# Query maxima of two attentions: split by query rows and turned in the score ring, in place of turned first and split after

## The reference

```
scores = q @ k.T * scale            # 1024 x 1024 for each batch and head
scores = scores + bias, causal mask # layer 1 only
attn   = softmax(scores, axis=-1)
y      = attn @ v                   # then a 128 x 128 output projection
```

## Time and profile before

| | before |
|---|---|
| time, median of 3 runs | 1030.89 us (1030.69 to 1034.01) |
| time of the profiled execution | 1036.33 us |
| its span in the profile | 1034.5 us |
| busy share of the span: PE, DVE, ACT, POOL | 87%, 78%, 59%, 19% |
| mean granted TensorE clock | 0.921 |
| L1025 DVE reductions of the first pass | 640, 488.3 us busy |
| L982 ACT exponentials of the second pass | 896, 436.3 us busy |
| L794 PE turns of maxima | 32 |
| L1000, L1002 DVE splits | 32 each |
| L560 transfers of maxima rows | 128 of 2.0 KB |

### The profile page before, as it was taken

How to read it: one execution, slowest core, us unless ns; L and a number is a source line. 1 busy time by engine, 2 the same in 40 slices (tenths; PEclk the granted TensorE clock), 3 DMA queues, 4 the chain that set the end, 5 groups by cost and what they waited for, 6 DMA issues and landing times. The chain is left out here.

```text
span 1034.5 us, 22166 instructions
## 1 busy us (share of the span) xinstructions
PE 899.6 (87%) x8501; PEld 458.8 (44%) x8501; DVE 805.0 (78%) x1600; ACT 612.7 (59%) x1280; POOL 199.8 (19%) x249
## 2 busy tenths in 40 slices
PE   5589999999899987984689999999998898777788
PEld 3212222222222223883345445555535666645568
DVE  7789999999899861656787787778862587799687
ACT  3228888888888786543236677766754346433552
POOL 2202033331302110540200011103010023133221
PEclk9659999999999898996779999999969998988899
DMA  2632435524426321111645753334301000000001
GB/s 77 186 87 61 118 95 124 101 70 94 99 76 146 96 60 19 50 35 49 177 99 141 188 104 87 88 73 88 68 7 30 6 1 2 1 0 1 4 6 36
DMA packets 62678, 73.71 MB, mean 71 GB/s; under 512 B 21144, under 2 KB 46865, under 8 KB 62559
## 3 DMA queue, kind: packets, MB, share of 16 engines
q1 hardware_dynamic: 48222, 49.23, 19.8%
q0 software_dynamic: 8576, 17.86, 7.2%
q10 hardware_dynamic: 5776, 5.22, 1.6%
HBM read 44.59 MB, written 18.16 MB: 61 GB/s over the span
## 5 line engine op out<-in xcount | busy, mean ns | idle before, releaser
L1025 DVE TENSOR_REDUCE a_negmax<-a_mbank 128x1 f32<-128x1024 f32 (+4 forms) x640 | 488.3, 818 | 72.7 <-PE a_mbank L829 35.2
L982 ACT ACTIVATE a_probs<-a_ebank 128x512 f32<-128x512 f32 (+3 forms) x896 | 436.3, 554 | 163.6 <-PE a_ebank L859 85.5
L850 PE MATMUL a_ebank<-b_moving,b_still 50*128 50x512 bf16 (+4 forms) x1280 | 270.0, 368 | 19.4 <-ACT a_probs L982 10.6
L821 PE MATMUL a_mbank<-a_moving,a_still 48*128 48x512 bf16 (+4 forms) x1280 | 263.3, 377 | 22.5 <-DVE a_negmax L989 9.8
L873 PE MATMUL a_acc<-a_probs,a_slot_v 128*32 128x512 f32 (+3 forms) x1792 | 224.9, 575 | 1.1 <-ACT a_probs L982 1.1
L850 PEld LDWEIGHTS a_ebank<-b_moving,b_still 58*64 58x64 bf16 (+1 forms) x1280 | 85.0, 102 | 254.0 <-ACT a_probs L982 198.6
L821 PEld LDWEIGHTS a_mbank<-a_moving,a_still 56*64 56x64 bf16 (+1 forms) x1280 | 69.3, 104 | 89.1 <-DVE a_negmax L1025 65.5
L859 PE MATMUL a_ebank<-a_bias_b,anti 64*64 64x176 bf16 (+4 forms) x1728 | 88.3, 231 | 0.0
L859 PEld LDWEIGHTS a_ebank<-a_bias_b,anti 64*64 64x64 bf16 x1728 | 69.6, 110 | 9.0 <-issue 0.2
L829 PE MATMUL a_mbank<-bias_a,anti 64*64 64x176 bf16 (+3 forms) x576 | 65.2, 238 | 0.0
L873 PEld LDWEIGHTS a_acc<-a_probs,a_slot_v 128*32 128x32 f32 x1792 | 35.8, 109 | 52.1 <-issue 42.0
(11 more groups left out here) (388 smaller groups left out, 1118.1 us busy)
## 6 DMA issues: line engine op xcount, KB each, us to landing
a_slot_v<-vo SPq DMA_DIRECT2D x16, 512.0 KB
b_moving<-stack SPq DMA_DIRECT2D x64, 96.0 KB
b_still<-stack SPq DMA_DIRECT2D x32, 192.0 KB
a_still<-stack SPq DMA_DIRECT2D x60, 96.0 KB, 2.8
a_moving<-stack SPq DMA_DIRECT2D x60, 96.0 KB, 2.9
expert<-in_expert_rows POOLq DMA_DIRECT2D x8, 578.0 KB, 4.0
a_bias_b<-trow SPq DMA_DIRECT2D x32, 66.0 KB
b_moving<-a_mparts SPq DMA_DIRECT2D x124, 2.0 KB
```

The source lines that it names most:

```text
L821: last = nc.tensor.matmul(mbank[COLS * c:COLS * (c + 1), bank, lo - left:hi - left], S.a_still[rows, q % 2, pr, at[c]:at[c] + COLS], S.a_m ...
L850: last = nc.tensor.matmul(ebank[COLS * c:COLS * (c + 1), s % NE, lo:512], S.b_still[rows, buf, pr, at:at + COLS], S.b_moving[rows, buf, h, ...
L982: nc.scalar.activation(probs[:, g % 2, j, lows[g]:512], ebank[:, s % NE, lows[g]:512], ACT.Exp).then_inc(p_full, 1)
L1025: nc.vector.tensor_reduce(to[:, at:at + 1], mbank[:, (index - 1) % NM, 0:right - left], AX.X, ALU.max, negate=True).then_inc(m_empty, 2 if ...
```

## The change

The maxima are split before they are turned. VectorE, still in the layout of query rows, rounds `negmax` (128 x 16) to bf16 in `upper` and subtracts in `lower`, both into `halves` (bf16). The two stand behind different units of the first pass (behind the 17th and 18th for h = 0), and L1030 moves to behind the next quad's first unit, `upper` and `lower` of h = 1 behind its second and third (in the second attention; one unit earlier in the first). TensorE multiplies `halves` by a bf16 identity into a bank of `ebank`, 32 x 128 (`turn_maxima`), at unit `TURN` (19 in the first attention, 21 in the second) and `LATE` (3 and 6). ScalarE copies it out as one step of the ring (`take_maxima`), and one transfer a side takes both parts, so 2 in place of 4. `mbank` holds units alone. The ring `ebank` is now numbered through the whole attention by a table of places, with no new start in each quad. The starts come out a little later: the first group of the first attention stands behind 24 units (23 so far), a steady quad of the second behind 48 (45 so far); its first quad keeps 32 units before the first group, and has 65 units before group 4 (61 so far).

```diff
-EARLY = [34, 39, 44, 49, 64]
+EARLY = [32, 37, 42, 47, 65]
...
-    uses = units[:2] + ["late"] + units[2:18] + ["turn"] + units[18:]
-    USES = len(uses)
-    LATE, TURN = uses.index("late"), uses.index("turn")
+    USES = len(units)
     NM, WIDE = (4, 512) if causal else (2, SEQ)
+    COMBINE = 1 if causal else 0
+    TURN, LATE, LAST = 17 + NM, 1 + COMBINE + NM, 1 + COMBINE
...
+    turned_at = {q * USES + TURN: (q, 0) for q in range(NQUAD)}
+    turned_at.update({(q + 1) * USES + (LATE if q + 1 < NQUAD else LAST): (q, 1) for q in range(NQUAD)})
...
+        for q in range(NQUAD):
+            for g in range(G):
+                n, middle, end = span(q, g)
+                place[q, g, 0], place[q, g, 1] = next(count), next(count)
+                maxima(n, middle)
+                place[q, g, 2], place[q, g, 3] = next(count), next(count)
+                maxima(middle, end)
...
         def load_maxima(eng, q, h, jj):
             row = 64 * jj + ROWS
-            return [eng.dma_start(S.b_moving[row + i:row + i + 1, q % 2, h], mparts[8 * jj:8 * (jj + 1), h, i, :])
-                    for i in range(2)]
+            return eng.dma_start(S.b_moving[row:row + 2, q % 2, h], mparts[2 * BT * jj:2 * BT * (jj + 1), h, :])
...
-                sp.wait_ge(m_empty, NM + q * USES + (TURN + 1))
+                sp.wait_ge(p_full, NE + place[q, 0] + 1)
                 load_rows(q, 0, range(2) if q else range(1))
...
-            def transpose_maxima(n, units_done, quads_done, h):
-
-                pe.wait_ge(m_empty, max(NM + units_done, n + 1))
-                if quads_done and causal:
-                    pe.wait_ge(combined, quads_done)
-                bank = n % NM
-                nc.tensor.transpose(mbank[0:2 * BT, bank, 0:P], negmax[:, h, :], S.ident[:]).then_inc(m_full, 1)
+            def turn_maxima(q, h):
+
+                step = place[q, h]
+                pe.wait_ge(lower_ready, 2 * q + (h + 1))
+                pe.wait_ge(p_full, step + 1)
+                nc.tensor.matmul(ebank[0:4 * BT, step % NE, 0:P], halves[:, h].rearrange("p j i t -> p (j i t)"), ident[:],
+                                 start=True, stop=True).then_inc(e_full, 1)
...
-                step = q * STEPS + s
-                pe.wait_ge(p_full, step + (NE if s == 0 and (STEPS - 1) % NE == 0 else 1))
+                pe.wait_ge(p_full, step + 1)
...
+            def take_maxima(q, h):
+
+                step = place[q, h]
+                act.wait_ge(e_full, step + 1)
+                if q:
+                    act.wait_ge(rows_loaded[h], q * 32)
+                nc.scalar.copy(mparts[:, h, :], ebank[0:4 * BT, step % NE, 0:P]).then_inc(p_full, 1)
+
+            take_maxima(0, 0)
+            act.wait_ge(p_full, NE + 1)
+            load_maxima(act, 0, 0, 1).then_inc(rows_loaded[0], 16)
...
+            def combine(q):
+                dve.wait_ge(m_empty, NM + (q + 1) * USES)
+                nc.vector.tensor_tensor(negmax[:, 1, :], negmax[:, 1, :], negmax2[:], ALU.min).then_inc(combined, 1)
...
+                nc.vector.tensor_copy(halves[:, h, :, 0, :], per_jj(negmax[:, h, :])).then_inc(upper_ready, 1)
...
+                    if q and causal and use == 0:
+                        combine(q - 1)
+                    if q and use == COMBINE:
+                        upper(q - 1, 1)
+                    if q and use == COMBINE + 1:
+                        lower(q - 1, 1)
+                    if use == 16:
+                        upper(q, 0)
+                    if use == 17:
+                        lower(q, 0)
```

160 lines of the change are left out of this document (80 added, 80 removed).

## The result

The changed kernel takes 1037.32 us (median of 20 runs, 1031.71 to 1043.38), the kernel before 1031.14 us beside it (20 runs, 1025.5 to 1044.35). The ratio is 1.0046, with a 95% interval of 1.0028 to 1.0065: slower, clear of no change, where 1013 and "faster" were forecast. The profiled execution took 1035.68 us (span 1033.9), against 1036.33 before (span 1034.5). So the two profiles lie 0.6 us apart and the medians 6.2: what a profile shows and what the medians show must be told apart here.

A forecast was written before the change was run, and what follows sets the result against it. TensorE and VectorE were taken to bound the first attention together, TensorE alone the second. Terms 0 - 4.0 - 2.5 + 1.2 + 2.3 - 9 + 0 - 6 = -18.0 us gave 1018.3 profiled, 1013 median, range 1003 to 1027.

The forecast's parts named there:

- Turns in the first attention: 15 turns in steady quads: a wait for ScalarE replaces the turn's own cost; 0 us, bounds -6.3 to +8.4.
- starts: Later group starts, weighed only as more units before group 4 of a first quad; 0 us, bounds -3 to +3.
- Restarts: Seven quad changes: the ring's full drain goes, 0.56 us of waiting each; -4.0 us, bounds 0 to -4.5.
- Rows of maxima: First attention: two transfers replace four, halving TensorE's 5.0 us wait for rows; -2.5 us, bounds 0 to -4.7.
- Opening of the first: First attention's opening: turn one unit later, first step moves from 69.95 to some 71.2; +1.2 us, bounds 0 to +2.5.
- Opening of the second: Second attention's opening: first turn waits for ScalarE's transfers until about 519; +2.3 us, bounds +1.0 to +4.0.
- Turns in the second: 14 steady turns in the second attention: idle before them goes, ring waits 0.1 each; -9 us, bounds -12 to -4.
- the text's own sign: Test for steady quads: wrong if quad-to-quad time in the second attention does not fall by some 1.2 us.
- The clock of the last quad: Last quad: no clock fall, so groups 1 to 6 take 14 us, not 20; -6 us, bounds 0 to -9.
- C: Rival: ring of three becomes the bound, each of 29 steady turns costing two 0.56 us waits; +11, 1042 us; chance 0.08.
- B: Rival: TensorE's gaps in the second attention are slack, restarts give half, clock stays; -3.5, 1027.5 us; chance 0.13.

The follow-up runs named there:

- e5: Changed kernel with the first attention's group starts one unit later and the second's old steady table moved by three units; 1029.63 us, ratio 0.9966.
- e2: Kernel before with only the ring of three banks counted on through all quads; 1030.89 us, ratio 0.9994.
- e13: Changed kernel with the first-pass unit reading rows 64 to 113 put first in each pair, both attentions; 1027.84 us, ratio 0.9944.
- e4: Changed kernel with each side's row pair moved by two transfers again instead of one; 1041.77 us, ratio 1.0076.
- e9: Changed kernel with the second pass's group starts one unit earlier in both attentions; 1025.98 us, ratio 0.9945.
- e11: Kernel before with every start of the second pass's groups one use later in both attentions; 1053.54 us, ratio 1.0199.
- e1: Changed kernel with the identity's cast issued after VectorE's eleventh reduction, only the first turn waiting for it; 1034.2 us, ratio 1.0009.
- e3: Changed kernel's split, single transfers and continuous ring, but the turn in mbank, copied by VectorE, and the identity's cast late; 1035.18 us, ratio 1.0032.
- e7: Changed kernel with the turns moved in their groups: one unit later in the first attention, behind fourth score steps in the second; 1038.45 us, ratio 1.0065.

## Why the prediction was wrong

The sum said -18.0 us for the profile. The profile moved by -0.6 and the median by +6.2. By the copy-outs above, and with the forecast in brackets, the profile moved by +0.35 up to the first one (+1.2), -0.80 in the first attention (-6.5), +3.83 from there to the first copy-out of the second (+2.3), +1.69 in the second up to its last quad (-9), -7.10 in the last quad (-6) and +1.43 in the rest of the program (0), which the change does not touch. Two steps of the text failed. The turns in the second attention gave back nothing, 10.7 us from the term, and the starts of the groups, set at 0, cost 8.0 us in the first. A third, carrying the clock's part over from one profile, is in the 6.8 us between the move of the profile and that of the median.

**Turns in the first attention, 0, and starts, 0.** The first is right: 2.83 us for the group, and e5 and e2 differ by 0.03 a half-quad. The second is the step that failed here. The text weighed only the starts of the second attention's first quad, and left out that the first attention's groups stand one unit later too. This sets which side each unit reads between the scores, and it cost 8.0 us (e5; 9.3 by e13), more than the 6.5 that restarts and rows were to give back. The trace of the kernel before held it, though no row read from it showed it: a score and a unit start together there, as in e13:

```profile
181.38 0.39 PE L850 MATMUL a_ebank<-b_moving,b_still 50*128 50x512 bf16 x1
181.38 0.39 PE L821 MATMUL a_mbank<-a_moving,a_still 48*128 48x512 bf16 x1
```

**Restarts, -4.0.** The 0.56 each was right (e2). Half the sum, 2.05, was left, since in the later quads other waits took the place.

**Rows of maxima, -2.5.** The 5.0 us of waiting went wholly, twice the term. The cause named, two transfers fewer, is not needed for it: no such wait stands in the profile with two transfers a side (e4), nor with the starts one unit earlier (e9), nor in the kernel before with its four transfers and the starts one later (e11). So each of several differences is enough to remove it; which one did so in the changed kernel stays open.

**Opening of the first, +1.2.** The first step came at 69.42 in place of the forecast 71.2, sooner than before; the first copy-out moved by 0.35.

**Opening of the second, +2.3.** The first step moved from 522.04 to 523.69, +1.65. Inside it the cast was taken at 0.2 and took 4.47, yet in the profile only ate the wait for ScalarE's queue that had been forecast (e1). Then the clock stayed low for longer (0.57 in 525 to 530, 0.88 before; 0.53 in 545 to 550, 0.83 before); the first copy-out came 3.4 later. Windows after:

```profile
540.00:545.00 5.00, 5.00 (x64) 2.41 (x57) 4.91 (x14) 2.26 (x5) 0.00 (x0) 0.50 1.01 184
545.00:550.00 5.00, 4.53 (x39) 1.45 (x35) 2.05 (x5) 2.88 (x7) 0.00 (x0) 0.53 0.97 300
```

**Turns in the second, -9.** This is the step of the text that failed outright, and the largest error: "some ring waits, which I set at 0.1 each". They are 7.1 us in 13, 0.55 each, nearly the 0.56 of the earlier trace rows, which the first attention's term had used. So of the 14.1 us that were to go almost whole, only 1.2 us of idle time and 1.0 of the turns' own went. Yet a quad, which by the text's own sign should have become 1.2 shorter, takes 0.46 more, and for this the runs give a lead and no cause. TensorE's idle time a quad hardly moved: in the windows from 563 to 746 us it is busy 173.66 of 183 before and 173.40 after, which is 29.1 of 30.71 and 29.5 of 31.17 us a quad. With other starts it is busy 30.2 a quad (e5), with the sides swapped 30.2 (e13), and with the sides as before 29.1 (e3). The sides do matter here, since swapping them alone makes a quad 0.37 longer (e13). But this busy time is modelled, and in e7, with starts and sides as in the changed kernel and only the turns moved, it is 29.9 in a quad of 31.10. So it cannot settle what the 0.46 are, and which order of sides is best here was not searched.

**The clock of the last quad, -6.** In the profile the mechanism came as forecast: no fall, and the two last steps gave 9.0 us, 7.8 of it in the step with the fall, less 1.9 in the one ahead (21.15 to 23.02). The gap behind the last turn is gone, and the one before it grew instead of shrinking:

```profile
754.62 0.23 PE L822 MATMUL a_ebank<-a_ident,a_halves 128*32 128x128 bf16 x1 [0.97 <-DVE a_halves L1041]
```

What failed is carrying it to the median. The clock of an execution goes with its time: of 111 executions of the kernel before, run beside the experiments, those at a clock of 0.922 or less have a median of 1036.7 us (23 of them), those at 0.931 or more 1028.0 (24). Its profiled execution had 0.921, and the median is 0.926; the changed kernel's is 0.931. And e2, whose second attention is that of the kernel before, falls to 0.78 and 0.54 in 750 to 760 but is back at 1.00 from 760 on, and its two last steps are 14.23 and 18.89, 4.3 us less than in the profile before. So part of those 9 us was the profiled execution's own. At 0.931 and above the changed kernel (12 executions) has 1035.5 us, 7.4 more than the one before: an estimate of what the change costs at a like clock, of which the changed kernel's higher clock gives some back. The fall near 344, which the text left in place, is absent from the changed kernel's profile, but e1's has one (0.66 in 340 to 345): such a fall belongs to an execution as much as to a kernel.

**Rivals.** C, the slower one, named the ring of three and was right that the exponential would be waited for, once a turn and not twice, and only in the second attention; but the ring alone does not make the kernel slower: e9 and e13 have the same one and are faster than the kernel before. B's thought, that gaps before a turn are slack, is nearest to what the second attention shows, and its half of the restarts is what e2 measured. The range of 1003 to 1027 missed the time because no case had the sides in it: with them put right and all else as in the changed kernel the medians are 1025.98 (e9), 1027.84 (e13) and 1029.63 (e5), about its upper end.

## What to carry to other kernels

When a change moves one instruction in a stream that interleaves two kinds of work on half of TensorE's rows each, look at which half meets which over the whole period, ahead of costing the instruction: here one unit's shift was worth 8 us of the first attention, and in the kernel before 13.5, where a wait for VectorE came on top. When a table of starts follows from a formula, try its neighbours by one and two; the best was one line away. And set a term that rests on a clock's fall against several executions, since one profile may hold a fall that the median lacks.

## What the hardware showed beyond expectation

A cast of 128 x 128 from float32 to bf16 on VectorE took 4.47 us beside GpSimd's addition of 4.49 us, 0.23 in the first attention without it and 0.21 when moved behind it (e1), while four reductions of 128 x 128 from PSUM ran beside the addition at 282 ns each, as long as the twelve behind it (e1). The Trainium skill (GPSIMD Engine Reference, Specifications) says that GpSimd shares its SBUF interfaces with VectorE and contends with instructions in a two-port mode or with two SBUF inputs; the cast has one SBUF input, and the trace agrees if it ran in the two-port mode, which no row shows.

Two matmuls on different sides started within 0.01 us of each other, two scores even ahead of the unit between them in the stream (183.20 above), and the sequence of sides alone moved the first attention from 310.26 to 300.92 us (e13).
